# State-space stage of a four-layer decoder: C is applied by ScalarE per token between two turns by TensorE, for 160 of 256 units

## The chip, the core and the metric

The kernel runs on one core of a Trainium2 chip (trn2). The metric is the device time of one execution in microseconds (us). The core has a matrix engine (TensorE, PE in the profile, its weight loads PEld), VectorE (DVE), ScalarE (ACT), GpSimd (POOL) and SyncE (SP), which here issues the DMAs. Each works through its own list of instructions in order and is coupled to the others by semaphores. TensorE writes to PSUM only; GpSimd does not read PSUM here.

## The reference

A decoder with four layers on x of 32 sequences x 64 tokens x 256 features (2048 tokens). Each layer adds an attention-like block, a second one and a feed-forward block to x. The change is in the first block of the third layer, a selective state-space block with 512 inner channels, 16 states per channel and a convolution over four tokens:

```python
dA = exp(A[None, :, None, :] * dt[:, :, :, None])
dBu = dt[:, :, :, None] * Bm[:, None, :, :] * hs[:, :, :, None]
def step(h, inp):
    dA_t, dBu_t, C_t = inp
    h = dA_t * h + dBu_t
    y = einsum('bdn,bn->bd', h, C_t)
    return (h, y)
y = y + hs * D[None, :, None]
y = y * silu(gate)
return einsum('bdl,hd->blh', y, Wout)
```

So for each channel d and state n there is a recurrence over the 64 tokens of a sequence; the state is multiplied by C of its token and of n, and summed over the 16 n.

## The kernel before

The function is `l2_attn` (L1415). Tokens are cut into four chunks q of 512 (8 sequences), the 512 channels into four groups c of 128 partitions. A **unit** u is one state n of one channel group of one chunk: a tile of 128 channels x 512 tokens. There are 4 x 4 x 16 = 256 units. 32 units make a **half** k (two channel groups cc = 0, 1 that alternate, 16 states), two halves a chunk; `split` (L1501) gives (k, n, cc).

For a unit: ScalarE makes the decay `da` = exp(dt x A) into PSUM (`decay`, L1617), GpSimd the input `ub` = dtu x B (L1721), with B copied to all partitions in `bcn` by a DMA from `bct`. VectorE runs the recurrence as one scan (L1783 or L1788). Then the state is multiplied by C, which is the other half of `bcn`. `pooled` (L1505) chooses who does it: for 80 units the scan writes SBUF (`hb`) and GpSimd multiplies (`product`, L1710, `hp`); for 176 the scan writes PSUM (`ph`), and VectorE, having waited for its own scan, multiplies into `hc` (L1792). In an even half 12 of 32 units are pooled, in an odd one 8. TensorE sums over n by a matmul with the identity that accumulates in `py` (L1608). After 16 states VectorE adds the skip term (`skip`, L1773), GpSimd multiplies by the gate (L1701).

The order of each engine is written out by `schedule` (L1518), which all engines call: before unit u it places the jobs that the table `AT` puts at this position of the chunk (0 to 63), shifted by each engine's own `after`. Jobs: H, the projection and convolution of the next chunk (TensorE at 2, 5, 8, 11; ScalarE and VectorE 5 later, three VectorE instructions each); O, the output projection of the last chunk (TensorE 14 and 17); S, silu of four tiles and of the gate on ScalarE with two loads of its tables (20), before which it makes the decays of units 20 to 23 into the SBUF tile `dx`; X, the projection to dt, B and C (TensorE 23 and 25); D, softplus of dt (31 to 40, GpSimd 8 later); Z, the gate's projection (43 to 52). In the first chunk Z and D jobs stand at the places of Y and O. The job X 1 writes B and C to `bcs`, which SP stores to DRAM for `bcn`.

How far the engines run ahead: `ub` has four buffers, so GpSimd's `ub` of unit u waits for scan u - 4; `product` of unit u is placed after `ub` of u + 2 and waits for scan u. ScalarE's decay of u waits for scan u - 2. `bcn` has four buffers, and SP waits for all that read one before it loads it again. `bank` (L1497) gives jobs one of two PSUM banks `pp` in turn.

Of the kernel before, what the change touches and what calls it, by code (L numbers as in the profile page):

```python
# [17 lines left out]
ALU = mybir.AluOpType  # L18
# [1396 lines left out]
def l2_attn(nc, g, a):  # L1415
# [4 lines left out]
    NB, NUB, NHC, NDX = 4, 4, 4, 4  # L1420
    NU = NQ * IC * N
    with ExitStack() as ctx:
# [11 lines left out]
        def early(sp):  # L1434
            for dst, n in loads:
# [12 lines left out]
        bcs = s.sb("bcs", [2 * N, CH])  # L1448
# [4 lines left out]
        hc = [s.sb(f"hc{k}", [P, CH]) for k in range(NHC)]  # L1453
# [10 lines left out]
         hc_ready, hp_ready, add_done, skip_done, zs_ready, yz_ready, o_ready) = s.sem(  # L1464
            "a_exp", "pp0_free", "pp1_free", "raw_ready", "tap_ready", "conv_ready", "hs_ready", "z_ready",
            "x_ready", "dtin_ready", "bc_ready", "bc_stored", "d_ready", "sp_ready", "m_ready", "dt_ready", "dtu_ready", "da_ready",
            "ub_ready", "scan_done", "hc_ready", "hp_ready", "add_done", "skip_done", "zs_ready", "yz_ready", "o_ready")
# [46 lines left out]
        by_dve = [u for u in range(NU) if not pooled(u)]  # L1514
        pool_count = [sum(x <= u for x in by_pool) for u in range(NU)]
        dve_count = [sum(x <= u for x in by_dve) for u in range(NU)]

        def schedule(job, unit, skip, after):  # L1518
# [3 lines left out]
            for u in range(NU):  # L1522
# [14 lines left out]
        with nc.Block() as block:  # L1537

            @block.sync
            def _(sp):  # L1540
# [7 lines left out]
                for i in range(NU // 2):  # L1548
# [5 lines left out]
                    if i >= NB:  # L1554
                        last = 2 * (i - NB) + 1
                        sp.wait_ge(ub_ready, last + 1)
                        sp.wait_ge(hc_ready, dve_count[last])
                        if pool_count[last]:
                            sp.wait_ge(hp_ready, pool_count[last])
# [3 lines left out]
            def _(pe):  # L1563
                pe.wait_ge(w_loaded, nl)

                def job(q, j):
# [12 lines left out]
                    elif kind == "X":  # L1579
# [4 lines left out]
                        mm.then_inc(x_ready, 1)  # L1584
                    elif kind == "D":
# [11 lines left out]
                def unit(u):  # L1597
                    k, n, cc = split(u)
                    if pooled(u):
                        pe.wait_ge(hp_ready, pool_count[u])  # L1600
                        src = hp[(pool_count[u] - 1) % 2]
                    else:
                        pe.wait_ge(hc_ready, dve_count[u])
                        src = hc[(dve_count[u] - 1) % NHC]
# [3 lines left out]
                    pe.matmul(py[:, turn_ % 2, :], g.ident[:, :], src[:, :], start=n == 0, stop=n == N - 1).then_inc(add_done, 1)  # L1608
# [4 lines left out]
            def _(act):  # L1613
# [9 lines left out]
                def job(q, j):  # L1623
# [19 lines left out]
                    elif kind == "X":  # L1643
# [4 lines left out]
                        else:  # L1648
                            if q:
                                act.wait_ge(bc_stored, 32 * q)  # L1650
                            act.activation(bcs[:, :], out[0:2 * N, :], ACT.Copy).then_inc(bc_ready, 1)
# [31 lines left out]
                schedule(job, unit, lambda t: None, {"H": 5, "X": 4, "D": 6, "Z": 5})  # L1683

            @block.gpsimd
            def _(pool):
# [39 lines left out]

                schedule(job, unit, gated, {"D": 8, "skip": 3})

            @block.vector
            def _(dve):  # L1730
# [44 lines left out]
                def unit(u):  # L1775
                    i = u // 2
                    dve.wait_ge(da_ready, u + 1)
                    dve.wait_ge(ub_ready, u + 1)
                    if pooled(u):
# [3 lines left out]
                        dve.tensor_tensor_scan(hb[m % 2][:, :], factor(u), ub[u % NUB][:, :], 0.0, ALU.mult, ALU.add).then_inc(scan_done, 1)  # L1783
# [1487 lines left out]
```

## Time and profile before

| | |
|---|---|
| median of 3 runs | 4679.01 us (4669.22 to 4682.99) |
| profiled execution | 4676.15 us, its span 4674.4 us |
| TensorE, weight loads | 3974.4 us (85%), 2613.4 us (56%) |
| VectorE, ScalarE, GpSimd | 3124.8 us (67%), 2221.0 us (48%), 1513.6 us (32%) |
| state-space units | 922.3 to 1462.2 us of the span |

Shares are those of the whole span; the stage that is changed is 540 us of it. PEclk in the rows below is the granted clock of TensorE, with 1.00 for 2.4 GHz and 0.5 for 1.2 GHz. In answers by line, "idle before" is the idle time of that engine just before such instructions, and the name behind the arrow ended it.

### The profile page before, as it was taken

The page shows a single profiled execution, that of the slowest core. Times are in us where ns is not written, and L with a number is a line of the kernel's source. Part 1 is how long each engine was busy: PE and PEld are TensorE (multiplying, and loading weights), DVE is VectorE, ACT ScalarE, POOL GpSimd, SP SyncE. Part 2 cuts the span into 40 slices and gives each one's busy share as a digit, 9 for nine tenths or more (in the row PEclk, how much of TensorE's full clock was granted, in tenths as well). Part 3 has the DMA queues.
Part 4 walks back from the last instruction along what each step waited for, and adds up shares of the span by engine and source line. Part 5 has one row for each costly group of instructions (what it writes and reads, how often), then busy time and mean ns, then how long its engine had stood idle before and what let it go on. Part 6 is the DMA issues. An engine that isn't in the chain of part 4 may idle for free. (4 is left out here: it accounts for less than half of the span.)

```text
span 4674.4 us, 143172 instructions
## 1 busy us (share of the span) xinstructions
PE 3974.4 (85%) x62052; PEld 2613.4 (56%) x62052; DVE 3124.8 (67%) x5769; ACT 2221.0 (48%) x4151; POOL 1513.6 (32%) x1605
## 2 busy tenths in 40 slices
PE   7627886677766887999899999999999998689999
PEld 6415654323324665344577777777777776355555
DVE  7897744788887887765577777777777776521111
ACT  3446532654443555322566666666666665221111
POOL 1001100088895221000444444444444442112222
PEclk9858997889998999999899999999999998789999
DMA  1000000133332000100200000001000000041111
GB/s 35 19 27 11 2 13 21 47 114 122 127 129 79 2 2 22 34 1 1 51 22 25 22 22 25 22 22 26 22 26 24 22 13 4 7 135 53 54 50 43
DMA packets 72969, 175.13 MB, mean 37 GB/s; under 512 B 14578, under 2 KB 27892, under 8 KB 69748
## 3 DMA queue, kind: packets, MB, share of 16 engines
q1 hardware_dynamic: 72340, 165.96, 11.3%
q8 instruction: 490, 8.03, 0.7%
q14 instruction: 139, 1.14, 0.1%
HBM read 163.04 MB, written 2.88 MB: 35 GB/s over the span
## 5 line engine op out<-in xcount | busy, mean ns | idle before, releaser
L1721 POOL TENSOR_TENSOR ssm_ub<-ssm_dtu,ssm_bcn 128x512 f32<-128x512 f32 x256 | 325.1, 1299 | 300.0 <-DMA ssm_bcn<-ssm_bct 297.6
L3085 DVE TENSOR_TENSOR moe_hh<-moe_si,moe_pu 128x512 f32<-128x512 f32 x104 | 71.4, 687 | 450.6 <-PE moe_pu L2974 444.3
L2526 POOL TENSOR_TENSOR dn_gm<-dn_cb,dn_cs 128x256 f32<-128x256 f32 x128 | 76.9, 622 | 670.1 <-DMA dn_cb<-dn_cum 439.1
L1620 ACT ACTIVATE ssm_da<-core_XN,ssm_al 128x504 f32<-128x504 f32 x240 | 163.2, 683 | 255.6 <-DVE ssm_ph L1788 169.9
L3018 ACT ACTIVATE moe_si<-moe_pg 128x512 f32<-128x512 f32 x104 | 62.1, 597 | 467.5 <-PE moe_pg L2974 467.5
L2542 POOL TENSOR_TENSOR dn_eb<-dn_ee,dn_cc 128x512 f32<-128x512 f32 x64 | 66.8, 1044 | 647.6 <-DVE dn_cc L2652 647.6
L3037 POOL TENSOR_TENSOR moe_hw<-moe_hh,moe_cb 128x512 f32<-128x512 f32 x100 | 126.8, 1268 | 444.1 <-DVE moe_hh L3085 393.6
L1608 PE MATMUL ssm_py<-ssm_hc,core_ident 128*128 128x512 f32 x352 | 200.0, 671 | 66.4 <-DVE ssm_hc L1792 35.8
L2293 PE MATMUL dn_po<-dn_wo,dn_cT 128*128 128x256 f32 x1024 | 244.8, 393 | 2.3 <-ACT dn_cT L2460 2.2
L2208 PEld LDWEIGHTS dn_pm<-dn_XB,dn_mb 32*32 32x32 f32 x16384 | 166.7, 105 | 113.3 <-issue 110.0
L2208 PE MATMUL dn_pm<-dn_zz,dn_XB 32*32 32x32 f32 x16384 | 209.3, 195 | 23.5 <-issue 23.5
L1788 DVE TENSOR_TENSOR_SCAN ssm_ph<-ssm_da,ssm_ub 128x512 f32<-128x512 f32 x168 | 205.0, 1220 | 29.9 <-POOL ssm_ub L1721 17.5
L347 POOL TENSOR_TENSOR a_ke<-a_qkT,a_kmask 128x512 f32<-128x512 f32 (+1 forms) x96 | 86.0, 917 | 411.2 <-DVEq L637 303.0
L2293 PEld LDWEIGHTS dn_po<-dn_wo,dn_cT 128*128 128x128 f32 x1024 | 194.1, 195 | 30.9 <-ACT dn_cT L2460 3.3
L2208 PE MATMUL dn_pm<-dn_XB,dn_mb 32*32 32x32 f32 x16384 | 196.9, 194 | 10.6 <-issue 9.0
L2974 PE MATMUL moe_pg<-core_XT,moe_w 128*128 128x512 f32 x416 | 198.4, 600 | 0.0
L2208 PEld LDWEIGHTS dn_pm<-dn_zz,dn_XB 32*32 32x32 f32 x16384 | 180.6, 104 | 28.6 <-issue 28.5
L2974 PE MATMUL moe_pu<-core_XT,moe_w 128*128 128x512 f32 x416 | 195.6, 592 | 0.0
L2989 PE MATMUL moe_py<-moe_w,moe_hw 128*128 128x256 f32 x800 | 188.7, 379 | 0.0
L2989 PEld LDWEIGHTS moe_py<-moe_w,moe_hw 128*128 128x128 f32 x800 | 152.0, 190 | 62.5 <-issue 46.9
L2557 POOL TENSOR_TENSOR dn_mb<-dn_BD,dn_small 128x256 f32<-128x256 f32 x256 | 178.8, 734 | 0.0
L560 ACT ACTIVATE a_sc<-a_sc 128x1024 f32<-128x1024 f32 (+1 forms) x128 | 121.2, 947 | 119.6 <-DVE a_sc L665 56.9
(504 smaller groups left out, 10527.2 us busy)
## 6 DMA issues: line engine op xcount, KB each, us to landing
ssm_bcn<-ssm_bct SPq DMA_DIRECT2D x128, 512.0 KB, 3.6
dn_cb<-dn_cum SPq DMA_DIRECT2D x32, 512.0 KB, 4.8
dn_w<-in_dn_w SPq DMA_DIRECT2D x32, 388.0 KB, 3.4
moe_cb<-moe_rows SPq DMA_DIRECT2D x64, 192.0 KB, 2.8
moe_w<-in_moe_w SPq DMA_DIRECT2D x26, 384.0 KB, 7.3
moe_cb<-moe_rows SPq DMA_DIRECT2D x64, 128.0 KB, 3.0
dn_wo<-in_dn_w SPq DMA_DIRECT2D x16, 256.0 KB, 5.9
moe_cb<-moe_rows SPq DMA_DIRECT2D x64, 64.0 KB, 2.6
```

Source lines behind the costliest of these rows:

```text
L347: last = pool.tensor_tensor(dst[:, c, :, :], bcm(src[:, c, :], R), bc(kmask[:, :], P), ALU.mult)
L560: act.activation(flat(sc[par][:, 2 * h:2 * h + 2, :]), flat(sc[par][:, 2 * h:2 * h + 2, :]), ACT.Exp, scale=sl)
L1608: pe.matmul(py[:, turn_ % 2, :], g.ident[:, :], src[:, :], start=n == 0, stop=n == N - 1).then_inc(add_done, 1)
L1620: act.activation(nb(factor(u))[:, :, 1:S], nb(dt[q % 2][:, c, :])[:, :, 1:S], ACT.Exp, scale=al[:, n, c:c + 1]).then_inc(da_ready, 1)
L1721: pool.tensor_tensor(ub[u % NUB][:, :], dtu[q % 2][:, c, :], bcn[i % NB][:, 0, :], ALU.mult).then_inc(ub_ready, 1)
L1788: dve.tensor_tensor_scan(ph[:, m % 2, :], factor(u), ub[u % NUB][:, :], 0.0, ALU.mult, ALU.add).then_inc(scan_done, 1)
L2208: mm = pe.matmul(bank[r, n * HB:(n + 1) * HB], left(n, r), right(n, r), start=True, stop=True, tile_position=(q * HB, q * HB))
L2293: mm = pe.matmul(po[:, j // 2, (j % 2) * D:(j % 2 + 1) * D], cT[:, h * TPC + j, :], wo[e // NCH % 2][:, h, :], start=h == 0, stop=h == 1)
L2557: last = pool.tensor_tensor(halves(mb[i % 2][:, l - 1, :]), BD[:, :, :], bcm(small[:, 1 + l, :], NS), ALU.mult)
L2974: mm = pe.matmul(dst[:, m % 2, :], w[:, k, at:at + P], g.XT[:, kc, n * CH:(n + 1) * CH], start=kc == 0, stop=kc == DC - 1)
L2989: mm = pe.matmul(py[:, j, 0:D], h[:, j * P:(j + 1) * P], w[:, k, DC * 2 * P:], start=k == 0, stop=k == G - 1)
L3037: pool.tensor_tensor(hw[m % 3][:, :], hh[m % 3][:, :], cb[j % NCB][:, :], ALU.mult).then_inc(hw_ready, 1)
```

## The change

160 units are now "turned" and 96 pooled (in each half those with number 0, 1, 4, 7, ... 31: `r < 2 or r % 3 == 1`). For a turned unit the scan writes one of two SBUF tiles `hu`. TensorE turns it (four 128x128 transposes into `ph`, so tokens lie on partitions), ScalarE copies it to SBUF in four pieces with C as the per-partition scale (`ht`, two buffers), and TensorE turns it back and sums in one step: four matmuls with the scaled piece as the stationary operand and the identity as the moving one, accumulating in `py`. C by tokens comes from a new job C in each chunk (TensorE at 28, ScalarE 4 later): four transposes of `bcs`, which is now 128 partitions high and cleared once by GpSimd, and a copy to `ct`. TensorE's unit u first turns u and then sums u - 2; ScalarE's unit u makes the decay of u and then scales u - 2. VectorE has no product any more. The skip is one unit later. The DMA queue no longer waits for `hc`.

```diff
         def pooled(u):
-            k, n, cc = split(u)
-            return cc == 1 and (n % 4 != 0 if k % 2 == 0 else n % 2 == 0)
+            r = u % (2 * N)
+            return r < 2 or r % 3 == 1
...
-                    if k and u % (2 * N) == 3 + cc + after.get("skip", 0):
+                    if k and u % (2 * N) == 4 + cc + after.get("skip", 0):
...
+                def turned(u):
+                    m = turn_count[u] - 1
+                    pe.wait_ge(scan_done, u + 1)
+                    if m >= 2:
+                        pe.wait_ge(ht_ready, m - 1)
+                    for j in range(TPC):
+                        mm = pe.transpose(ph[:, m % 2, j * P:(j + 1) * P], hu[m % NHU][:, j * P:(j + 1) * P], g.ident[:, :])
+                    mm.then_inc(turned_done, 1)
+                def summed(u):
...
+                    m = turn_count[u] - 1
+                    pe.wait_ge(ht_ready, m + 1)
+                    for j in range(TPC):
+                        mm = pe.matmul(py[:, cc, j * P:(j + 1) * P], ht[m % NHT][:, j * P:(j + 1) * P], g.ident[:, :],
+                                       start=False, stop=n == N - 1 and j == TPC - 1)
+                    mm.then_inc(add_done, 1)
+                def unit(u):
+                    if not pooled(u):
+                        turned(u)
+                    if u >= 2:
+                        summed(u - 2)
...
+                def scaled(u):
+                    if u < 0 or pooled(u):
+                        return
+                    k, n, cc = split(u)
+                    m = turn_count[u] - 1
+                    act.wait_ge(turned_done, m + 1)
+                    if m >= NHT:
+                        act.wait_ge(add_done, by_turn[m - NHT] + 1)
+                    for j in range(TPC):
+                        last = act.activation(ht[m % NHT][:, j * P:(j + 1) * P], ph[:, m % 2, j * P:(j + 1) * P], ACT.Copy,
+                                              scale=ct[k // 2 % 2][:, j, n:n + 1])
+                    last.then_inc(ht_ready, 1)
                 def unit(u):
+                    ahead_of(u)
+                    scaled(u - 2)
...
                     else:
-                        m = dve_count[u] - 1
-                        if m >= 2:
-                            dve.wait_ge(hc_ready, m - 1)
-                        dve.tensor_tensor_scan(ph[:, m % 2, :], factor(u), ub[u % NUB][:, :], 0.0, ALU.mult, ALU.add).then_inc(scan_done, 1)
-                        if m >= NHC:
-                            dve.wait_ge(add_done, by_dve[m - NHC] + 1)
-                        dve.wait_ge(scan_done, u + 1)
-                        dve.tensor_tensor(hc[m % NHC][:, :], ph[:, m % 2, :], bcn[i % NB][:, 1, :], ALU.mult).then_inc(hc_ready, 1)
+                        m = turn_count[u] - 1
+                        if m >= NHU:
+                            dve.wait_ge(turned_done, m - NHU + 1)
+                        dst = hu[m % NHU]
+                    dve.tensor_tensor_scan(dst[:, :], factor(u), ub[u % NUB][:, :], 0.0, ALU.mult, ALU.add).then_inc(scan_done, 1)
```

## Rows read from the trace of the kernel before

**Rows 1.** Busy us of each engine in windows cut at the skips, us from span's start.

```profile
922.30:1003.00 80.70, 60.67 (x118) 22.95 (x118) 68.08 (x72) 40.00 (x58) 69.09 (x54) 0.86 0.36 119
1003.00:1070.00 67.00, 45.48 (x86) 16.45 (x86) 57.60 (x64) 31.69 (x48) 62.77 (x51) 0.91 0.35 129
1070.00:1140.10 70.10, 55.13 (x130) 24.88 (x130) 63.75 (x69) 31.68 (x45) 59.32 (x46) 0.94 0.34 118
...
1207.40:1279.50 72.10, 56.65 (x130) 24.80 (x130) 63.80 (x69) 31.59 (x45) 59.33 (x46) 0.92 0.32 115
...
1346.40:1407.20 60.80, 41.09 (x96) 18.36 (x96) 54.61 (x57) 26.06 (x36) 58.42 (x45) 0.92 0.38 135
1407.20:1462.20 55.00, 39.24 (x64) 12.96 (x64) 50.93 (x56) 18.49 (x27) 46.96 (x39) 0.86 0.33 115
sum 539.90, PE 390.51 PEld 153.95 DVE 473.82 ACT 242.85 POOL 481.40; mean PE 48.81 PEld 19.24 DVE 59.23 ACT 30.36 POOL 60.17
```

In each window the columns are its length, then PE, PEld, DVE, ACT and POOL, the granted clock, DMA share and GB/s.

**Rows 2.** Groups by line in 917 to 1462 us, shapes kept apart, VectorE.

```profile
L1788 DVE TENSOR_TENSOR_SCAN ssm_ph<-ssm_da,ssm_ub 128x512 f32<-128x512 f32 x168 | 205.0, 1220 | 29.9 <-POOL ssm_ub L1721 17.5 <-issue 11.2 <-ACT ssm_da L1620 1.1
L1792 DVE TENSOR_TENSOR ssm_hc<-ssm_ph,ssm_bcn 128x512 f32<-128x512 f32 x176 | 121.8, 692 | 19.1 <-DVE ssm_ph L1788 1.4
L1783 DVE TENSOR_TENSOR_SCAN ssm_hb<-ssm_da,ssm_ub 128x512 f32<-128x512 f32 x72 | 87.5, 1215 | 10.4 <-ACT ssm_da L1620 4.6 <-POOL ssm_ub L1721 4.0 <-issue 1.9
```

**Rows 3.** GpSimd's waits for scans in an even window (1070 to 1140.1) and an odd one.

```profile
POOL ssm_hp L1710 <- DVE ssm_hb L1783: 11.6, 5, 3.3
...
POOL ssm_hp L1710 <- DVE ssm_hb L1783: 1.9, 3, 0.7
```

**Rows 4.** Order of time in a quiet stretch: start us, us, engine, what.

```profile
1047.86 4.96 POOL L1721 TENSOR_TENSOR ssm_ub<-ssm_dtu,ssm_bcn 128x512 f32<-128x512 f32 x4
...
1050.33 1.22 DVE L1788 TENSOR_TENSOR_SCAN ssm_ph<-ssm_da,ssm_ub 128x512 f32<-128x512 f32 x1
...
1052.26 1.21 DVE L1783 TENSOR_TENSOR_SCAN ssm_hb<-ssm_da,ssm_ub 128x512 f32<-128x512 f32 x1
...
1053.39 1.21 DVE L1788 TENSOR_TENSOR_SCAN ssm_ph<-ssm_da,ssm_ub 128x512 f32<-128x512 f32 x1
```

**Rows 5.** Order of time: an X job (512 columns), transposes, f32 matmuls of 128 columns.

```profile
1119.63 3.60 PE L1583 MATMUL ssm_pp<-ssm_hs,ssm_wx 128*128 128x512 f32 x8
...
2345.52 0.80 PEld L2279 LDWEIGHTS dn_po<-core_ident,dn_cn 128*128 128x128 f32 x7 [0.29 <-issue]
...
21.53 1.86 PEld L378 LDWEIGHTS a_pm<-core_XT,a_wqk 128*128 128x128 f32 x16 [1.06 <-ACTq L579]
```

**Rows 6.** Groups of activations by line, shapes kept apart.

```profile
L2475 ACT ACTIVATE dn_sqr<-dn_bC 128x128 f32<-128x128 f32 x64 | 17.8, 277 | 44.9 <-PE dn_bC L2315 44.8
L1628 ACT ACTIVATE ssm_acc<-ssm_pp,ssm_vec 128x512 f32<-128x512 f32 x13 | 8.8, 679 | 6.0 <-PE ssm_pp L1577 6.0
L1666 ACT ACTIVATE ssm_zs<-ssm_pp 128x512 f32<-128x512 f32 x16 | 9.3, 583 | 4.0 <-PE ssm_pp L1577 4.0
L1620 ACT ACTIVATE ssm_dx<-core_XN,ssm_al 128x504 f32<-128x504 f32 x16 | 10.1, 699 | 0.0
```

**Rows 7.** Order of time: a convolution on VectorE and the scan after it.

```profile
942.99 2.34 DVE L1747 SCALAR_TENSOR_TENSOR ssm_acc<-ssm_pp,ssm_vec,ssm_acc 128x504 f32<-128x504 f32 x3
945.64 1.23 DVE L1788 TENSOR_TENSOR_SCAN ssm_ph<-ssm_da,ssm_ub 128x512 f32<-128x512 f32 x1 [0.31 <-POOL ssm_ub L1721]
```

**Rows 8.** Order of time: first and last part of a silu job on ScalarE.

```profile
1106.25 2.52 ACT L1620 ACTIVATE ssm_dx<-core_XN,ssm_al 128x504 f32<-128x504 f32 x4
...
1114.46 1.28 ACT L1642 ACT_TABLE_LOAD   x1
```

**Rows 9.** Order of time: an output job on TensorE.

```profile
1106.90 3.62 PE L1594 MATMUL ssm_pp<-ssm_wout,ssm_yy 128*128 128x256 f32 x16
```

**Rows 10.** Busy us in two windows, columns as in the first group.

```profile
965.00:985.00 20.00, 12.06 (x18) 4.46 (x18) 13.76 (x13) 15.05 (x20) 16.47 (x11) 0.66 0.23 79
1106.00:1122.00 16.00, 12.41 (x37) 6.67 (x36) 14.44 (x15) 11.67 (x15) 12.83 (x8) 1.00 0.28 99
```

More of the change, by code:

```diff
@@ L1419, in l2_attn @@
     NQ = TOK // CH
-    NB, NUB, NHC, NDX = 4, 4, 4, 4
+    NB, NUB, NHU, NHT, NDX = 4, 4, 2, 2, 4
     NU = NQ * IC * N
@@ L1447, in l2_attn @@
         dtin = s.sb("dtin", [P, CH])
-        bcs = s.sb("bcs", [2 * N, CH])
+        bcs = s.sb("bcs", [P, CH])
+        ct = [s.sb(f"ct{k}", [P, TPC, N]) for k in range(2)]
         bcn = [s.sb(f"bcn{k}", [P, 2, CH]) for k in range(NB)]
@@ L1452, in l2_attn @@
         hb = [s.sb(f"hb{k}", [P, CH]) for k in range(2)]
-        hc = [s.sb(f"hc{k}", [P, CH]) for k in range(NHC)]
+        hu = [s.sb(f"hu{k}", [P, CH]) for k in range(NHU)]
+        ht = [s.sb(f"ht{k}", [P, CH]) for k in range(NHT)]
         hp = [s.sb(f"hp{k}", [P, CH]) for k in range(2)]
@@ L1513, in l2_attn @@
         by_pool = [u for u in range(NU) if pooled(u)]
-        by_dve = [u for u in range(NU) if not pooled(u)]
+        by_turn = [u for u in range(NU) if not pooled(u)]
         pool_count = [sum(x <= u for x in by_pool) for u in range(NU)]
-        dve_count = [sum(x <= u for x in by_dve) for u in range(NU)]
+        turn_count = [sum(x <= u for x in by_turn) for u in range(NU)]
         def schedule(job, unit, skip, after):
@@ L1556, in _ @@
                         sp.wait_ge(ub_ready, last + 1)
-                        sp.wait_ge(hc_ready, dve_count[last])
                         if pool_count[last]:
@@ L1584, in job @@
                         mm.then_inc(x_ready, 1)
+                    elif kind == "C":
+                        pe.wait_ge(bc_ready, q + 1)
+                        if q == 0:
+                            pe.wait_ge(bcs_zeroed, 1)
+                        for j in range(TPC):
+                            mm = pe.transpose(out[:, j * P:(j + 1) * P], bcs[:, j * P:(j + 1) * P], g.ident[:, :])
+                        mm.then_inc(c_ready, 1)
                     elif kind == "D":
@@ L1650, in job @@
                                 act.wait_ge(bc_stored, 32 * q)
-                            act.activation(bcs[:, :], out[0:2 * N, :], ACT.Copy).then_inc(bc_ready, 1)
+                            else:
+                                act.wait_ge(bcs_zeroed, 1)
+                            act.activation(bcs[0:2 * N, :], out[0:2 * N, :], ACT.Copy).then_inc(bc_ready, 1)
+                        act.drain().then_inc(free, 1)
+                    elif kind == "C":
+                        out, free, uses = bank(q, j)
+                        act.wait_ge(c_ready, q + 1)
+                        act.activation(ct[q % 2][:, :, :], out.rearrange("p (j r) -> p j r", j=TPC)[:, :, N:2 * N], ACT.Copy)
                         act.drain().then_inc(free, 1)
@@ L1681, in unit @@
                     decay(u)
-                schedule(job, unit, lambda t: None, {"H": 5, "X": 4, "D": 6, "Z": 5})
+                schedule(job, unit, lambda t: None, {"H": 5, "X": 4, "C": 4, "D": 6, "Z": 5})
             @block.gpsimd
@@ L1725, in unit @@
                         product(u)
+                pool.memset(bcs[:, :], 0.0).then_inc(bcs_zeroed, 1)
                 schedule(job, unit, gated, {"D": 8, "skip": 3})
```

32 lines of the change are left out of this document (18 added, 14 removed).

## The prediction

> **What bounds the kernel now.** I began with the busy time of each engine in the state-space stage, cut where VectorE runs the skip of a half (unit 3 of the next half) [rows 1]. The reader should see two engines near their limit and two with room: over the 539.9 us from the first `ub` to the last skip GpSimd is busy 481.4 us and VectorE 473.8, TensorE 390.5, ScalarE 242.9. The even windows, with convolution, silu and output jobs, have VectorE above GpSimd (63.8 against 59.3 of 70.1 us); the odd ones, with the softplus jobs, have GpSimd above VectorE (62.8 against 57.6 of 67.0). Next came the groups by line [rows 2]: 176 products `hc` take 121.8 us of VectorE, 256 scans about 320. Then what GpSimd waits for [rows 3]: 11.6 us in an even window, always a scan whose product it must make, and 1.9 in an odd one. Last, a quiet stretch in order of time [rows 4]: a scan whose product VectorE makes takes 1.93 us until the next scan starts (1050.33 to 1052.26), a scan alone 1.13 (1052.26 to 1053.39); four `ub` take 4.96 us with the last one's tail, a pitch of 1.23. So the stage is bound by VectorE in even windows and by GpSimd in the softplus part of odd ones. Removing VectorE work pays at most in the first kind.
>
> **What goes, comes and moves.** VectorE loses all 176 products and the waits on its own scan: a turned unit's scan now costs 1.13 us instead of 1.93. The scans write SBUF where 168 wrote PSUM; those that already do so last 1.215 us against 1.220 [rows 2], so I cost that at nothing. VectorE's work falls by about 16 us a half and it no longer bounds an average half.
>
> GpSimd gains 16 products (96 for 80), 16 x 1.23 = 20 us. Where they land matters. In an odd window there were 7 and will be 12: +5 x 1.23 = 6.1. An even window had 13 and gets 12: -1.2. The first gets one more, the last (28 units) two more.
>
> TensorE: a unit had two instructions of 512 columns; eight such take 3.60 us with the last one's tail, so I take 0.43 each and 0.86 a unit [rows 5]. Now it has four transposes and four f32 matmuls of 128 columns. Seven transposes' weight loads span 0.80 us, a pitch of 0.11, so four take 0.44 (result after some 0.75); sixteen loads of f32 matmuls of this form span 1.86 us, also 0.11, and the four are eight instructions, 0.89. Together 1.33 us, +0.47, so 160 x 0.47 = 75 us of work on an engine with 149 us of idle time, all at full clock.
>
> ScalarE: 640 scalings of 128x128 from PSUM with a per-token scale. No row has this form. Without a scale operand it is 277 ns; 128x512 from PSUM costs 679 with one and 583 without, so the operand adds 0.09; I take 0.37 us each. Chained activations overlap: four of 0.699 take 2.52 [rows 8], so by 0.09 each. Four scalings are then 4 x 0.37 - 3 x 0.09 = 1.21 us, 1.12 of occupation [rows 6]. Bounds: 4 x 0.277 - 0.27 = 0.84, and without overlap 1.48. In all 160 x 1.12 = 179 us beside 242.9: ScalarE becomes 78% busy. What VectorE did for a unit in 0.69 us ScalarE does in 1.21. The Trainium skill (ScalarE: Activation LUTs, Rules for kernel authors) says to put `mul` on VectorE, not ScalarE; counted product for product that rule would give +160 x 0.52 = +83 us, some 4762. The rows do not support adding it up like that, since ScalarE idles for half of every window.
>
> Small edits: GpSimd's clearing of `bcs` sits in its 297 us of idle time before the first `ub`; the four C jobs add four transposes and a 0.6 us copy each, beside GpSimd work; the DMA queue loses a wait. Nothing.
>
> **Where the waits go.** In a quiet run of three units (two turned, one pooled) the demands are GpSimd 4 x 1.23 = 4.9 us, ScalarE 3 x 0.63 + 2 x 1.12 = 4.1, TensorE 2 x 1.33 + 0.86 = 3.5, VectorE 3.4. GpSimd bounds; an odd window becomes 62.8 + 6.1 + 1.2 of issue gaps and semaphore waits + 0.5 at the skip = 70.6 us, against 66.9 to 67.3: +3.5 in each of three. The last window: 47.0 + 2.5 + some 3.8 at the end = 53.3 against 55.0, -1.7.
>
> Even windows. (a) A convolution takes 2.65 us of VectorE (942.99 to 945.64) [rows 7] before each of four pooled scans, so three units need 3.4 + 2.65 = 6.05 us of VectorE against 4.9 of GpSimd. GpSimd must wait at each product; the first wait is covered by its lead of two units, the other three are 1.2 each: 3.6. (b) The silu job keeps ScalarE 9.5 us (1106.25 to 1115.74) [rows 8], and now the scalings of two older units queue behind it. From the end of scan 17: TensorE turns unit 17 only after the second output job, 3.6 us [rows 9]; the turned state is there at 3.4, scaled at 4.6; silu until 14.1; unit 18 scaled at 15.3, unit 20 at 16.4; unit 21 could be turned only after the sum of unit 18, so it is scaled at 18.1; then the decay of unit 24 at 18.8 and scans 24 and 25 end at 20.0 and 21.1. GpSimd comes to the product of unit 25 at 16.1 and waits 5.0. (c) Two X jobs of 3.6 us [rows 5] stand in TensorE's queue before units 23 and 25; the turns behind them hold ScalarE's scalings and with them the next decays. Carried on in the same way GpSimd loses 5 us more up to unit 33. In all 3.6 + 10 + 1 at the skip = 14.6 us, where it waited 11.6 (and about the same 2 us more in the other such window). So 59.3 - 1.2 + 14.6 = 72.7 against 70.1 and 72.1: +2.6 and +0.6. The first window has Z jobs instead of output jobs: 69.1 + 1.2 + 0.5 + 12.6 = 83.4 against 80.7, +2.7. The seventh has neither convolution nor X: 58.4 - 1.2 + 4 = 61.2 against 60.8, +0.4.
>
> Sum: 2.7 + 3 x 3.5 + 2.6 + 0.6 + 0.4 - 1.7 = +15 us. (d) TensorE would idle about 8 us while it waits for unit 18's scaling. In the window 965 to 985, where it waited in the same place, the granted clock was 0.66, with stretches at 1.2 GHz; in the corresponding 1106 to 1122, where it kept its sums coming, it was 1.00 at 2.4 GHz [rows 10]. Half clock would hit the X jobs: 3.4 us lost for 6.8 us at half clock, of which GpSimd's four buffers hide part; I take 2 us in each of three: +6. Bounds 0 and +15. Total +21. The profiled execution took 4676.2 us (2.8 under the median of 4679.0), so it would take 4697; against the median, 4700.
>
> **Rivals.** *Unchanged waits.* The gates above are loose by a microsecond each; if GpSimd's waits and gaps stay near 45 us (58.5 now), the stage takes 501 + 45 = 546, +6: 4685. For it: GpSimd runs up to four units ahead. Against: ScalarE's queue order, with scalings behind silu, is fixed. *Faster.* With VectorE off the path only GpSimd's own work remains: 481.4 + 19.6 + 20 of ends, gaps and convolution waits = 521, -19: 4660. It needs the silu job and the X jobs to be hidden by the lead of GpSimd; the point is total waits under about 25 us. The old even windows, where these jobs cost VectorE only some 2.6 us of idle time, speak for it; that a turned unit now makes three more hand-overs between engines before its buffer is free speaks against. *ScalarE bounds.* If small activations do not overlap, three units cost 3 x 0.69 + 2 x 1.48 = 5.0 us plus jobs, above GpSimd; some 0.4 us a triple and longer silu tails give +55: 4735. *TensorE at half clock.* Its work is 160 x 1.33 + 96 x 0.86 + some 105 of jobs = 400 us at full clock; with half clock for 60% of the work it needs 640 and sets the stage: +100, 4780. The matmuls proper in three units fall little, from 2.6 us in some 5.3 to 2.6 in 4.9, so rows do not show a reason. The Trainium skill (TensorE: Matmul & The Clock Gate, Part 4: PE-mode transpose) says that transposes do not count as activity for the clock; no stretch here is pure enough to test that, and by it this rival would be the likelier the more time goes to turns.
>
> **How the numbers follow.** About 0.3% (14 us) is what a measurement of this kernel can tell from no change. Forecast (coupled queues, 4700) 0.42; ScalarE or TensorE as the bound 0.10; unchanged waits 0.34; faster 0.14. The time is the forecast's. The range takes in the unchanged case, the near end of faster (4665), the unlucky ends of (b) to (d) and ScalarE's case: 4665 to 4742; that leaves out most of faster and the half-clock case. Slower 0.52, same 0.34, faster 0.14.
>
> **What would show it.** GpSimd busy near 501 us of a stage of about 561; its waits for scans in even windows about 15 us, longest (5 us) after the silu job; odd windows near 70.6 us; VectorE busy about 350; a scaling 0.37 us; turns with a pitch of 0.11; a TensorE wait of some 8 us for scaled states in each silu job, with a lower granted clock after it. It would be wrong if odd windows stay at 67, if the waits vanish, or if TensorE or ScalarE is without idle time in the quiet stretches.

## The result and the profile after

The changed kernel takes 4711.6 us (median of 5 runs, 4704.7 to 4719.8) against 4679.0 (5 runs, 4664.6 to 4683.0): ratio 1.0071, with 95% between 1.0052 and 1.0090, so 33 us slower. The forecast was 4700 and its range 4665 to 4742. Whether the way there was the forecast one is another matter, and the windows answer it.

The first part of the page, busy time of each engine, of the changed kernel; its profiled execution took 4711.6 us with a span of 4709.8:

```profile
PE 4027.0 (86%) x63660; PEld 2776.6 (59%) x63668; DVE 3018.6 (64%) x5593; ACT 2383.1 (51%) x4795; POOL 1529.6 (32%) x1622
```

The same windows as in [rows 1], of the changed kernel, cut at the first skip of each half, with the same columns:

```profile
919.80:1028.50 108.70, 75.39 (x324) 47.33 (x324) 56.43 (x51) 60.78 (x143) 70.17 (x54) 0.84 0.26 89
1028.50:1096.60 68.10, 54.05 (x288) 39.25 (x288) 41.86 (x38) 52.55 (x129) 66.71 (x56) 0.92 0.37 124
1096.60:1169.40 72.80, 61.80 (x332) 44.21 (x332) 51.95 (x50) 51.92 (x126) 60.56 (x48) 0.93 0.34 117
1169.40:1237.40 68.00, 51.49 (x288) 36.57 (x288) 41.91 (x38) 52.44 (x129) 66.62 (x55) 0.97 0.36 124
1237.40:1309.80 72.40, 61.36 (x332) 44.06 (x332) 51.98 (x50) 51.92 (x126) 60.56 (x48) 0.95 0.35 118
...
1377.80:1441.00 63.20, 51.27 (x296) 41.24 (x296) 43.22 (x37) 46.12 (x115) 57.51 (x48) 0.89 0.40 134
1441.00:1493.60 52.60, 40.32 (x260) 31.73 (x260) 37.05 (x33) 38.31 (x104) 50.48 (x42) 0.96 0.37 121
sum 573.80, PE 445.74 PEld 319.79 DVE 366.29 ACT 406.47 POOL 499.22; mean PE 55.72 PEld 39.97 DVE 45.79 ACT 50.81 POOL 62.40
```

The stage grew by 33.9 us, from 539.9 to 573.8, which is all of the loss. Of that 28.0 lie in the first window (80.7 to 108.7) and 5.9 in the other seven. The busy sums are what was expected of a change that moves work: GpSimd 499 us, VectorE 366, ScalarE 406. In the first window no engine is near its limit: TensorE is busy 75 and GpSimd 70 of 109 us. That points to engines that wait for each other in a ring rather than to one that bounds. In the odd windows GpSimd is now the bound (66.7 of 68.1).

The groups of the changed kernel by line, shapes kept apart:

```profile
L1716 ACT ACTIVATE ssm_ht<-ssm_ph,ssm_ct 128x128 f32<-128x128 f32 x640 | 182.4, 376 | 97.6 <-PE ssm_ph L1611 96.4
L1846 DVE TENSOR_TENSOR_SCAN ssm_hu<-ssm_da,ssm_ub 128x512 f32<-128x512 f32 x148 | 179.9, 1219 | 94.0 <-ACT ssm_da L1650 79.3 <-POOL ssm_ub L1778 12.9 <-PE ssm_ph L1611 1.2
```

A scaling lasts 376 ns. The scans stand idle 79 us for decays, and the reason is one line up: ScalarE, which makes the decays, stands 96 us in front of a scaling until TensorE has turned the state. Where? The waits in the first window:

```profile
ACT ssm_ht L1716 <- PE ssm_ph L1611: 41.7, 12, 6.6
DVE ssm_hu L1846 <- ACT ssm_da L1650: 41.3, 14, 5.2
...
POOL ssm_hp L1767 <- DVE ssm_hb L1846: 25.2, 7, 6.2
...
PE ssm_pp L1578 <- DVEq L1808: 11.1, 3, 3.7
```

And one round of it in order of time:

```profile
949.83 3.63 PE L1578 MATMUL ssm_pp<-core_XT,ssm_win 128*128 128x512 f32 x4 [3.69 <-DVEq L1808]
949.96 1.23 DVE L1846 TENSOR_TENSOR_SCAN ssm_hb<-ssm_da,ssm_ub 128x512 f32<-128x512 f32 x1 [0.32 <-issue]
...
951.26 1.26 POOL L1767 TENSOR_TENSOR ssm_hp<-ssm_hb,ssm_bcn 128x512 f32<-128x512 f32 x1 [6.10 <-DVE ssm_hb L1846]
...
953.30 0.60 PE L1611 MATMUL ssm_ph<-core_ident,ssm_hu 128*128 128x128 f32 x4
...
953.94 1.14 ACT L1716 ACTIVATE ssm_ht<-ssm_ph,ssm_ct 128x128 f32<-128x128 f32 x4 [6.62 <-PE ssm_ph L1611]
...
955.43 0.71 ACT L1650 ACTIVATE ssm_da<-core_XN,ssm_al 128x504 f32<-128x504 f32 x1
...
955.62 1.98 PE L1578 MATMUL ssm_pp<-core_XT,ssm_win 128*128 128x512 f32 x4 [0.82 <-ACT ssm_zs L1703]
...
956.17 1.22 DVE L1846 TENSOR_TENSOR_SCAN ssm_hu<-ssm_da,ssm_ub 128x512 f32<-128x512 f32 x1 [4.99 <-ACT ssm_da L1650]
...
960.97 2.33 DVE L1805 SCALAR_TENSOR_TENSOR ssm_acc<-ssm_pp,ssm_vec,ssm_acc 128x504 f32<-128x504 f32 x3
...
963.48 3.64 PE L1578 MATMUL ssm_pp<-core_XT,ssm_win 128*128 128x512 f32 x4 [3.69 <-DVEq L1808]
```

The first chunk has Z jobs between the H jobs (TensorE at 2 H, 3 Z, 5 H, 6 Z, ...), and jobs take the two `pp` banks in turn. So H 1 needs the bank of H 0 (in later chunks it is H 2 that does), and VectorE frees that only with its convolution, which stands before unit 7 in its own order. TensorE has H 1 before unit 5 and so stops there. Now follow the rows: the job starts when the convolution has ended (949.83), and the turn of the unit that has its place behind the job ends 4 us later (953.30 and 0.60); ScalarE's scaling of that unit had stood at the head of its queue for 6.6 us; the next decay comes only behind it (955.43), so VectorE's scan starts at 956.17, idle for 5.0; and the next convolution, which frees the next bank, stands behind that scan (960.97). Each convolution thus waits for the job that waited for the one before. From one such job to the next three units take 13.65 us (949.83 to 963.48), where the kernel before took 7.64 (942.99 [rows 7] to its next convolution at 950.63).

The clock takes a part of each round. The four matmuls that start at 949.83 take 3.63 us, the four of the same form at 955.62 take 1.98. Windows of the changed kernel around the first of them, columns as above, show the granted clock at 0.53, near the 1.2 GHz level, behind the wait of 3.69 us, and at 1.00 (2.4 GHz) in the next stretch:

```profile
949.80:953.40 3.60, 3.57 (x5) 1.51 (x6) 1.23 (x1) 0.00 (x0) 2.14 (x2) 0.53 0.03 5
953.40:957.60 4.20, 3.38 (x19) 2.18 (x18) 1.22 (x1) 2.20 (x6) 1.70 (x3) 1.00 0.32 125
```

So some 1.65 us of the 13.65 (3.63 less 1.98) are the slower clock, and they lie on the ring, since the turn stands behind this job.

### The profile page after: what moved, and what is told of

Same layout as the page of the kernel before. It is cut to its first block and busy times, and to the rows that moved or that the text cites. A ratio compares the mean times of both kernels' runs of the same rounds, so it can differ in the third digit from the quotient of the medians.

```text
span 4709.8 us, 147050 instructions
## 1 busy us (share of the span) xinstructions
PE 4027.0 (86%) x63660; PEld 2776.6 (59%) x63668; DVE 3018.6 (64%) x5593; ACT 2383.1 (51%) x4795; POOL 1529.6 (32%) x1622
## 5 line engine op out<-in xcount | busy, mean ns | idle before, releaser
L2596 POOL TENSOR_TENSOR dn_eb<-dn_ee,dn_cc 128x512 f32<-128x512 f32 x64 | 66.7, 1042 | 651.3 <-DVE dn_cc L2706 651.3
L1846 DVE TENSOR_TENSOR_SCAN ssm_hu<-ssm_da,ssm_ub 128x512 f32<-128x512 f32 x148 | 179.9, 1219 | 94.0 <-ACT ssm_da L1650 79.3
L2262 PEld LDWEIGHTS dn_pm<-dn_XB,dn_mb 32*32 32x32 f32 x16384 | 166.6, 105 | 110.9 <-issue 107.5
L1716 ACT ACTIVATE ssm_ht<-ssm_ph,ssm_ct 128x128 f32<-128x128 f32 x640 | 182.4, 376 | 97.6 <-PE ssm_ph L1611 96.4
L1627 PEld LDWEIGHTS ssm_py<-core_ident,ssm_ht 128*128 128x128 f32 x1280 | 170.2, 201 | 68.2 <-issue 40.1
L1627 PE MATMUL ssm_py<-core_ident,ssm_ht 128*128 128x128 f32 x1280 | 177.5, 285 | 26.0 <-ACT ssm_ht L1716 26.0
```

The lines of the kernel that those rows point to most:

```text
L1627: mm = pe.matmul(py[:, cc, j * P:(j + 1) * P], ht[m % NHT][:, j * P:(j + 1) * P], g.ident[:, :], start=False, stop=n == N - 1 and j == TPC ...
L1716: last = act.activation(ht[m % NHT][:, j * P:(j + 1) * P], ph[:, m % 2, j * P:(j + 1) * P], ACT.Copy, scale=ct[k // 2 % 2][:, j, n:n + 1])
L1846: dve.tensor_tensor_scan(dst[:, :], factor(u), ub[u % NUB][:, :], 0.0, ALU.mult, ALU.add).then_inc(scan_done, 1)
L2262: mm = pe.matmul(bank[r, n * HB:(n + 1) * HB], left(n, r), right(n, r), start=True, stop=True, tile_position=(q * HB, q * HB))
```

## The experiments

Eleven kernels, all measured against the kernel before. The ratios are taken over the repeated runs, the stage and the windows are of one profiled execution of each kernel. Window lengths are cut as above: first, second (odd), third (even), seventh.

| kernel | pooled | ratio (95%) | stage us | first | 2nd | 3rd | 7th |
|---|---|---|---|---|---|---|---|
| before | 80 | 1 | 539.9 | 80.7 | 66.9 | 70.2 | 60.8 |
| changed | 96 | 1.0071 (1.0052 to 1.0090) | 573.8 | 108.7 | 68.1 | 72.8 | 63.2 |
| e1 Z jobs ahead | 96 | 1.0015 (1.0002 to 1.0028) | 547.3 | 82.4 | 68.0 | 72.7 | 63.2 |
| e2 the same in before | 80 | 1.0004 (0.9993 to 1.0016) | 543.5 | 82.3 | 66.9 | 72.2 | 60.8 |
| e3 turn first | 96 | 1.0018 (1.0004 to 1.0031) | 552.8 | 91.2 | 68.0 | 72.9 | 60.2 |
| e4 scalings in silu | 96 | 1.0049 (1.0032 to 1.0067) | 562.5 | 105.5 | 68.0 | 68.7 | 63.2 |
| e5 before, new set | 96 | 1.0033 (1.0020 to 1.0046) | 553.2 | 83.5 | 66.9 | 76.3 | 60.3 |
| e7 e1+e3+e4 | 96 | 0.9973 (0.9961 to 0.9985) | 531.6 | 81.2 | 68.0 | 67.1 | 60.2 |
| e8 e7, fewer | 72 | 0.9989 (0.9972 to 1.0006) | 532.4 | 83.9 | 65.4 | 70.1 | 58.6 |
| e9 e7, fewer in odd | 84 | 0.9976 (0.9959 to 0.9993) | 523.5 | 81.4 | 65.7 | 66.1 | 60.2 |
| e10 e7, shifted | 96 | 0.9994 (0.9983 to 1.0005) | 538.5 | 83.2 | 68.0 | 67.8 | 61.8 |
| e11 e5, shifted | 96 | 1.0005 (0.9995 to 1.0016) | 546.1 | 81.2 | 67.0 | 74.5 | 60.6 |
| e12 e9, shifted even | 84 | 0.9977 (0.9965 to 0.9989) | 528.4 | 83.4 | 65.7 | 67.8 | 61.2 |

### Is it the bank ring? e1 and e2

e1 does the four Z jobs of the first chunk before unit 0, as the H jobs already are, and changes nothing else; e2 does that to the kernel before, as a control.

```diff
-        ahead = [("H", 0), ..., ("X", 1), ("D", 1), ("C", 0)]
+        ahead = [("H", 0), ..., ("X", 1), ("D", 1), ("C", 0), ("Z", 0), ("Z", 1), ("Z", 2), ("Z", 3)]
...
-        AT.update({("Y", c): 3 + 3 * c for c in range(IC)})
```

> The changed kernel, with the four gate projections of the first chunk (Z jobs of chunk 0) done before unit 0 instead of between units 3 and 12. Theory A (ring through the PSUM banks): in the first half TensorE comes to the projection H 1 at unit 5 and needs the bank that VectorE's convolution of H 0 frees only before unit 7; the turn of unit 5 is queued behind it, ScalarE's scaling behind the turn, the decay of unit 8 behind the scaling. Without the Z jobs the banks alternate over two more units, as in the later chunks, and the first half falls from 108.7 us to some 80 to 85: about 4686 us. Theory B (the first half simply has more TensorE work and a lower clock, 0.84): only the work of the Z jobs goes, four times 1.9 us, so at most 8 us: about 4704. Theory C (two buffers of hu and ht are too few): no change but those 8 us.

> The same edit in the kernel before, as a control. Theory A: TensorE waits for the banks there too, but only sums are queued behind, with four buffers of hc, so no ring closes: the first half falls from 80.7 us by the 3 to 6 us that TensorE's extra work cost at most, about 4674 us. Theory B: a similar gain in both kernels, some 8 us each.

e1: the first window falls from 108.7 to 82.4 us, the stage by 26.5, and the ratio from 1.0071 to 1.0015, which is 26 us. First its window, then its waits in the same place:

```profile
921.90:1004.30 82.40, 65.80 (x319) 43.28 (x317) 55.48 (x51) 61.28 (x144) 70.29 (x55) 0.88 0.34 117
```

```profile
DVE ssm_hu L1845 <- ACT ssm_da L1649: 13.4, 9, 4.0
...
ACT ssm_ht L1715 <- PE ssm_ph L1610: 11.8, 8, 4.5
POOL ssm_hp L1766 <- DVE ssm_hb L1845: 9.4, 7, 1.9
```

GpSimd does the same work (70.2 and 70.3 us), and the wait of `hu` scans for decays falls from 41.3 to 13.4. TensorE has less to do in the window, since the Z jobs, 16 matmuls that now take 7.0 us in one piece, run before it; e2 (no gain from the same move) and e3 (most of the gain without it) below show that this is not what was gained. The wait of `ssm_pp` for VectorE's queue is no longer among them. In order of time, turns of e1 with the H job between them, and two convolutions:

```profile
937.84 0.60 PE L1610 MATMUL ssm_ph<-core_ident,ssm_hu 128*128 128x128 f32 x4
...
941.36 1.88 PE L1577 MATMUL ssm_pp<-core_XT,ssm_win 128*128 128x512 f32 x4
...
943.08 0.60 PE L1610 MATMUL ssm_ph<-core_ident,ssm_hu 128*128 128x128 f32 x4
...
948.32 0.60 PE L1610 MATMUL ssm_ph<-core_ident,ssm_hu 128*128 128x128 f32 x4
...
949.01 2.33 DVE L1804 SCALAR_TENSOR_TENSOR ssm_acc<-ssm_pp,ssm_vec,ssm_acc 128x504 f32<-128x504 f32 x3
...
955.01 2.33 DVE L1804 SCALAR_TENSOR_TENSOR ssm_acc<-ssm_pp,ssm_vec,ssm_acc 128x504 f32<-128x504 f32 x3
```

TensorE passes three units in 5.24 us at first (937.84 to 943.08 to 948.32) and then settles to VectorE's round: from one convolution to the next it is 6.00 us (949.01 to 955.01) instead of 13.65. Four convolutions make three such rounds, so 3 x 7.65 = 23 of the 26.3 us that this window lost are explained by the round alone. It is the bank wait that set it. e2 shows that the edit is worth nothing by itself: in the kernel before the same wait existed, but only sums stood behind it on TensorE, and `hc` had four buffers. Of the kernel before:

```profile
953.15 1.98 PE L1577 MATMUL ssm_pp<-core_XT,ssm_win 128*128 128x512 f32 x4 [1.37 <-DVEq L1750]
```

I had expected 3 to 6 us from the first window of e2 and got 82.3 for 80.7, so no gain shows from removing the few `pp` waits there (3.9 us in three waits for convolutions). e2 says one more thing: its third window is 72.2 us where the kernel before had 70.2, though the edit does not reach it. A single window can thus differ by 2 us between two profiles.

### Is it the turn's place behind the job? e3

The wait for the bank can also be left alone if the turn goes ahead of the job in TensorE's order. Nothing else moves, and the buffers are the same.

```diff
-        def schedule(job, unit, skip, after):
+        def schedule(job, unit, skip, after, first=lambda u: None):
...
                 q, at = u // (IC * N), u % (IC * N)
+                first(u)
...
                 def turned(u):
+                    if pooled(u):
+                        return
...
-                    if not pooled(u):
-                        turned(u)
...
-                schedule(job, unit, lambda t: None, {})
+                schedule(job, unit, lambda t: None, {}, turned)
```

> The changed kernel, with TensorE's turn of unit u placed ahead of the jobs at u instead of behind them; the sum of u - 2 stays behind. Nothing else. Theory A: the bank wait no longer holds a turn, so the ring opens: first half from 108.7 us to 85 or 90, and the even halves lose 1 to 3 us each of waits behind O and X jobs; about 4685 us. Theories B and C: the work, clock and buffers are the same, so 4711 within 3 us.

The first window is 91.2 us: 17.5 of the 28 come back although the bank wait remains. Of e3, in the same stretch as above:

```profile
949.70 1.98 PE L1579 MATMUL ssm_pp<-core_XT,ssm_win 128*128 128x512 f32 x4 [1.53 <-DVEq L1809]
...
951.13 1.26 POOL L1768 TENSOR_TENSOR ssm_hp<-ssm_hb,ssm_bcn 128x512 f32<-128x512 f32 x1 [3.80 <-DVE ssm_hb L1847]
```

```profile
949.70:958.45 8.75, 7.22 (x35) 4.59 (x35) 5.66 (x6) 5.10 (x15) 4.95 (x4) 1.00 0.15 60
```

TensorE now waits 1.5 us for the bank where it waited 3.7, and GpSimd 3.8 where it waited 6.1; a round takes 8.75 us (turns at 943.66 and 952.41). The clock stays at 1.00 through the round, and the job behind the wait takes 1.98 us where it took 3.63, so up to 1.65 of the 4.9 us that each round gains come with the clock: e3 by itself does not separate it from the order. Both links, the bank and the place of the turn, belong to the ring, and cutting the bank wait (e1) cuts it best. The third link, ScalarE's scalings ahead of its decays, is read from the trace alone: no run moved it. The seventh window fell from 63.2 to 60.2, which was not expected; the gain expected in the other even windows didn't come (72.9 for 72.8): there something later in the half seems to take it up. e4 and e7 below fit that: with the silu job mended too, this edit is worth 1.6 and 2.6 us in these windows (67.1 and 66.1 in e7, 68.7 in e4).

### What holds the even windows: e4

The scalings of units 18, 20 and 21 stand behind the silu job. e4 puts them between its activations.

```diff
                             act.activation(zs[(q - 1) % 2][:, :, :], zs[(q - 1) % 2][:, :, :], ACT.Silu).then_inc(zs_ready, 1)
+                            base = (q - 1) * IC * N + silu_at
+                            scaled(base - 2, True)
...
                                 act.activation(hs[q % 2][:, k, :], acc[:, k, :], ACT.Silu, bias=tap(K, k)).then_inc(hs_ready, 1)
+                                if q and k in (1, 3):
+                                    scaled(base + k // 2, True)
...
-                def scaled(u):
-                    if u < 0 or pooled(u):
+                def scaled(u, now=False):
+                    if u < 0 or pooled(u) or (u in early and not now):
```

> The changed kernel, with ScalarE's scalings of the pending units (18, 20, 21 of each chunk) put between the silu activations instead of behind the whole silu job. Theory S (GpSimd's 4.2 us wait after the silu job comes from the scalings queued behind it): that wait and TensorE's 7.5 us wait for scaled states go, 3 to 4 us in each of four chunks: about 4698 us. Rival: the wait only moves to the two X jobs of TensorE that come next, so at most 1 us a chunk: 4708.

The silu job in the changed kernel, in order of time:

```profile
1129.63 2.54 ACT L1650 ACTIVATE ssm_dx<-core_XN,ssm_al 128x504 f32<-128x504 f32 x4
...
1137.85 1.28 ACT L1672 ACT_TABLE_LOAD   x1
1139.15 2.17 ACT L1716 ACTIVATE ssm_ht<-ssm_ph,ssm_ct 128x128 f32<-128x128 f32 x8
...
1140.34 2.07 PE L1627 MATMUL ssm_py<-core_ident,ssm_ht 128*128 128x128 f32 x8 [7.49 <-ACT ssm_ht L1716]
...
1145.05 1.22 DVE L1846 TENSOR_TENSOR_SCAN ssm_hu<-ssm_da,ssm_ub 128x512 f32<-128x512 f32 x1 [6.48 <-ACT ssm_da L1650]
...
1147.47 1.26 POOL L1767 TENSOR_TENSOR ssm_hp<-ssm_hb,ssm_bcn 128x512 f32<-128x512 f32 x1 [4.15 <-DVE ssm_hb L1846]
```

Eight scalings in a row at 1139.15 end a wait of 7.5 us of TensorE, and GpSimd's product pays 4.15. In e4 the same stretch reads:

```profile
1132.74 1.91 ACT L1665 ACTIVATE ssm_zs<-ssm_zs 128x2048 f32<-128x2048 f32 x1
1134.56 1.12 ACT L1725 ACTIVATE ssm_ht<-ssm_ph,ssm_ct 128x128 f32<-128x128 f32 x4
1135.56 1.34 ACT L1676 ACTIVATE ssm_hs<-ssm_acc,ssm_vec 128x512 f32<-128x512 f32 x2
...
1135.73 1.22 PE L1627 MATMUL ssm_py<-core_ident,ssm_ht 128*128 128x128 f32 x8 [3.61 <-ACT ssm_ht L1725]
```

The even windows fall from 72.8 and 72.4 to 68.7, the stage by 11.3 us and the ratio by 0.0022, 10 us. So the scalings behind silu are worth some 4 us in each, as much as GpSimd's wait there. The expectation had four chunks of 3 to 4 us and 4698; it came to 4695.9, with 3.2 us in the first window and nothing in the seventh.

### Is the new set of pooled units to blame? e5 and e11

e5 is the kernel before with the new choice of pooled units alone; e11 the same with the choice one place earlier, so that the products stand elsewhere beside the convolutions.

```diff
         def pooled(u):
-            k, n, cc = split(u)
-            return cc == 1 and (n % 4 != 0 if k % 2 == 0 else n % 2 == 0)
+            r = u % (2 * N)
+            return r < 2 or r % 3 == 1
```

(e11: `r % 3 == 0`.)

> The kernel before, with only the new choice of pooled units (96 for 80, the products of the other 160 still on VectorE). It measures the share that GpSimd's extra work has by itself. By the prediction's terms GpSimd gains 16 x 1.23 = 20 us, nearly all in odd halves, where VectorE, which loses 16 x 0.8 = 13 us, is not the bound during the softplus jobs but is elsewhere: +1 to +4 us in each odd half, 0 to -2 in the even ones, about 4682 us. Rival: that GpSimd's work is hidden and VectorE's relief pays, about 4665.

> The kernel before with 96 pooled units in the shifted set 0, 1, 3, 6, ... 30 (products of the others on VectorE). With 0, 1, 4, 7, ... 31 its even halves grew from 70.2 and 72.1 us to 76.3 and 76.5, although the number of products there was the same, 12. If the convolutions before pooled scans are the cause, they go back to 70 to 73 and the kernel to about 4680. If it is the pooling of both channel groups in turn (sums of both wait for GpSimd), they stay at 76.

Both missed. In e5 the odd windows don't move (66.9 and 67.2) although a half of them has 12 products instead of 8, and the even ones grow by 6.1 and 4.4 us, to 76.3 and 76.5, where a half has 12 in both. The even window of e5 and its waits:

```profile
1078.00:1154.00 76.00, 60.49 (x130) 25.94 (x130) 64.38 (x70) 31.48 (x45) 60.64 (x47) 0.87 0.32 112
```

```profile
ACT ssm_da L1620 <- DVE ssm_hb L1783: 18.9, 8, 3.9
...
POOL ssm_hp L1710 <- DVE ssm_hb L1783: 15.4, 7, 3.4
```

VectorE's work is what it was [rows 1], and GpSimd waits 15.4 us for scans where it waited 11.6 [rows 3]. The shift of e11 brings back some 2 us (74.5 and 73.9), no more than a window can differ between profiles; in the ratios, 1.0033 and 1.0005, the shift is clearer. What makes the rest was not found. What e5 does show: had VectorE kept its product for the other 160 units, the new set by itself would cost 13 us of stage, and the changed kernel with its ring cured (e1) stands at 547.3 against e5's 553.2. With this set TensorE and ScalarE in VectorE's place are therefore no loss. Against the shifted set (e11, 546.1) they are no gain either.

### The cures together, and the number of pooled units: e7 to e10, e12

e7 is e1, e3 and e4 at once; its e4 part names unit 19 too, which is pooled in e7 but turned in some of the others. The rest change its choice of pooled units alone:

```diff
-            return r < 2 or r % 3 == 1
+            return r < 2 or r % 4 == 1                                # e8
+            return r < 2 or r % (4 if u // (2 * N) % 2 else 3) == 1   # e9
+            return r < 2 or r % 3 == 0                                # e10
```

e12 is e9 with `r % 3 == 0` in even halves.

> The changed kernel with the three edits together: Z jobs of the first chunk ahead, the turn ahead of the jobs, scalings between the silu activations. If the ring and the silu queue are what the change costs, their gains add except where the first two open the same ring: 29.5 and 30.3 us share most, the third gives 15.7, so 4711.6 - 31 - 15 = 4665, and GpSimd is left as the bound with waits under 15 us. If another engine had become the bound underneath, it stays at or above 4675.

> As the one with all three edits, with 72 pooled units (0, 1, 5, 9, ... 29 of each half) and 184 turned. If GpSimd is the bound after the mends, 24 products less take 24 x 1.23 = 29 us off it, of which TensorE (24 x 0.47 = 11 us more) and ScalarE (24 x 1.14 = 27 us more) give some back in even halves: about 4650. If ScalarE and TensorE are level with GpSimd already, no gain or a loss: 4665 to 4680.

> As the one with all three edits, with the smaller pooled set in odd halves only (84 pooled, 172 turned). In odd halves GpSimd has the softplus jobs and bounds with 66.7 of 68 us, while ScalarE and TensorE wait: 12 products less, 12 x 1.23 = 15 us, should come off nearly in full: about 4651. In even halves nothing changes. If it equals the run with 72 pooled units, the even halves are bound by ScalarE and TensorE.

> As the one with all three edits and 96 pooled units, but the pooled ones are 0, 1, 3, 6, ... 30 instead of 0, 1, 4, 7, ... 31. The four convolutions of an even half stand before units 7, 10, 13, 16: with the old set each stands just before a pooled scan, whose product GpSimd waits for; now before a turned one. If that coincidence costs its waits (5.5 us of GpSimd in an even half of the run with all three edits), three of four even halves lose 2 to 4 us: stage 531.6 to some 522, about 4655. If the convolution is then only waited for at the next product: no change, 4663.

> All three edits, the shifted set in even halves and 0, 1, 5, 9, ... 29 in odd ones (84 pooled). By the stage of the runs so far (531.6 us with 96, 522.6 with 84) and 3 us less in each of three even halves: stage about 514 against 539.8 before, about 4652, so faster than the kernel before by 0.4 to 0.5%. If the shift gives nothing, 4660.

e7 beats both kernels: 4662.9 us, ratio 0.9973 (0.9961 to 0.9985). Its third window, and GpSimd's waits in it:

```profile
1072.50:1139.60 67.10, 62.94 (x335) 43.55 (x333) 51.81 (x51) 52.11 (x127) 60.53 (x48) 0.97 0.37 127
```

```profile
POOL ssm_hp L1777 <- DVE ssm_hb L1856: 5.5, 5, 1.5
```

GpSimd waits 5.5 us there for scans instead of 10.1, and TensorE is busy 62.9 of 67.1: it now stands level with GpSimd. TensorE also keeps its clock there: its wait in the silu job is 0.97 us. Fewer pooled units (e8) don't help in even windows: 70.1, with GpSimd busy only 55.5 us and more turns on TensorE (62.7) and ScalarE (55.1). None of them is at its limit, so it is the chain of turns that is likely longer; no run shows it. e8 missed: 4668 us where 4650 was expected. Fewer in odd windows alone (e9) do help: 68.0 to 65.7, and the stage is 523.5, 16 us under before. Its median doesn't show all of that (4662.1 where 4651 was expected; the ratio of 0.9976 is 11 us). The shifted sets (e10, e12) missed as well: their even windows are 67.8 against 67.1 and 66.1, and e10's ratio (0.9994) is above e7's (0.9973), so the place of the convolutions beside the products is not what is left there.

One reading limits all of this. The span minus the stage, which no edit touches but the one that puts the Z jobs ahead, was 4134.6 us in the profile of before, 4136.1 in that of the changed kernel, and between 4124.3 (e11) and 4149.3 (e8) in the others. Over the kernels that is a range of 25 us, so a gain of some 10 us in the stage can be lost in the whole. e7, e9 and e12 are each faster than before; which of them is best was not settled.

## Why the prediction was right, and where it was not

- **The sum and its sign.** 4711.6 against 4700, inside the range, and slower as forecast; the number was good by luck. Of the 33.9 us of stage, 28.0 lie in one window priced at +2.7, a term too small by 25.3. Without the ring (e1) the stage is +7.4, where the sum had +15 and 6 more for the clock. So two errors of opposite sign made the number look good.
- **The first window (+2.7, was +28.0): the failed step.** The text treated it as an even window with "Z jobs instead of output jobs". It took each job at its length and never asked which bank a job takes and who frees it. The bank waits were in the trace of before (the job of 1.98 us above that began when VectorE's queue had freed its bank) and cost nothing there, as e2 shows, since only sums stood behind them. The change put the turns there, and with ScalarE's scalings in front of its decays the wait went round. e1 and e3 show the bank and the turn's place as links; the link through ScalarE is in the rows (5.0 us of idle time of a scan until the decay that followed the scaling), without a run of its own. The slower clock behind each bank wait, some 1.65 us a round, was not in the term either. How the prediction came to 12.6 us of waits in this window it does not say.
- **Odd windows (+3.5 each, were +1.2, +0.7 and +1.1).** GpSimd bounds them, as said, with 1.4 us of idle time (68.10 less 66.71) where 1.7 was taken. Its busy time was too high: 68.9 expected, 66.7 measured. An odd half now has 54 GpSimd operations (32 `ub`, 12 products, 10 others), and 54 x 1.235 us is 66.7. Before it had 8 products, so 50 operations, which is 61.7; the window was busy 62.8 [rows 1], so it held about one more than its own. The sum took the 7 products that this window happened to hold and added five where four come (1.2 us), to a busy time with one too many (1.0 us). Products should have been counted by the rule in the code, not by the window.
- **Even windows (72.7 expected, 72.8 and 72.4).** Right in length, by terms that traded places; the base itself moved by 2 us between two profiles (e2), so the +2.6 of the first is not sharp. The terms: busy 60.6 where 58.1 was expected (an even half keeps its 12 products, so nothing was to be taken off, and the window holds 48 operations where 46 were), waits 12.3 (10.1 and 2.2) where 14.6 was. In order of time GpSimd waits 2.3 us at the products behind convolutions (3.6 expected; 0.2, 1.04 and 1.04), 4.15 behind the silu job (5.0), 5.8 from there to the end of the X jobs (5) and nothing at the skip (1). TensorE's wait for scaled states was 7.5 us (8).
- **Seventh window (+0.4, was +2.4), last (-1.7, was -2.4).** The seventh's excess is the turn behind its jobs, as e3 shows (60.2).
- **The clock (+6).** TensorE waited as foreseen, and the granted clock there was 0.68 where it had been 1.00 [rows 10]:

```profile
1129.00:1145.00 16.00, 7.97 (x41) 6.25 (x40) 8.19 (x5) 13.95 (x28) 14.32 (x9) 0.68 0.25 101
```

  The loss has the size of the term: from the end of the wait to the X job (1140.34 to 1145.45) TensorE needs 5.1 us for a turn and three sums that take 3.1 at full clock (0.44, 0.86 and twice 0.89), so 2.0. But it falls on these and not on the X jobs, which ran at 3.60 us each as before. e4 gives little of it back, though the clock of its even windows is 0.98 for 0.93. The same work behind the shorter wait takes 4.9 us (1135.73 to 1140.59) at a granted clock of 0.65:

```profile
1135.70:1140.60 4.90, 4.87 (x23) 3.83 (x24) 2.15 (x2) 4.88 (x13) 4.90 (x4) 0.65 0.12 35
```

  What rose is mostly the clock of the time in which TensorE waited (0.59 from 1132.8 to 1140.3 in the changed kernel), and that costs nothing. The half-clock rival fell: with 160 turned units the odd windows were granted 0.92, 0.97 and 0.97 (0.91, 0.88 and 0.91 before).
- **Costs.** A scaling 376 ns (0.37 taken), four in 1.14 us (1.21), GpSimd busy 499 us (501), a scan into SBUF 1219 ns (as before): these held. ScalarE gained 164 us (179), TensorE 55 (75). VectorE kept 366 us (350): its 121.8 us of products had in part overlapped their neighbours, and 107.5 left.
- **Rivals.** "Unchanged waits" had +6 of stage; with the first chunk cured it is +7.4, so that rival describes the stage without the ring better than the forecast does (+5.9 in the other seven windows, +12.3 in its sum). "Faster" needed the silu and X jobs to be hidden; they were not, though e4 and e7 show they can be in part. ScalarE was never the bound (406 of 574 us). The rule of the Trainium skill (ScalarE: Activation LUTs, Rules for kernel authors) that puts `mul` on VectorE was the ground for a time of 4762. In speed the trace agrees with it: 1.14 us for a unit on ScalarE against 0.69 on VectorE. But that time did not come on top where ScalarE has room; e7 is faster than the kernel before with all 640 scalings on ScalarE.

## What to carry to other kernels

When a step is moved into an engine's fixed order, list what that engine waits for just ahead of the new place, in the first round of the loop too, and follow each wait to the engine that ends it; if that one now needs the moved step, the waits form a ring, and its round can cost far more than any term of work (13.65 us here for three units of 6.00). A window in which every engine is a third idle is how it looked in this profile. Cutting one link of the ring was enough to bring back most of it. A helper copy in an in-order queue belongs between the long jobs, not behind them, and a window's busy time should be checked against its own count of operations before a term is added to it.

## What the hardware showed that was not expected

Transposes among f32 matmuls did not lower TensorE's clock. The Trainium skill (TensorE: Matmul & The Clock Gate, Part 4: PE-mode transpose) says that the full clock does not engage for transposes, since they do not count as busy in the same way. The odd windows, in each of which 20 units are now turned, were granted 0.92, 0.97 and 0.97 of full clock with TensorE busy 50 to 54 of 68 us, against 0.91, 0.88 and 0.91 before (45 to 47 of 67 us). With 23 turned in each (e9) it was 0.97, 0.97 and 0.95. Each turned unit has its f32 matmuls too, so this says that the mixture keeps the clock, not what transposes alone would do.

The same job shows in two kernels what a wait of TensorE can do to its clock: behind a bank wait of 3.69 us four matmuls took 3.63 us at a granted clock of 0.53, behind one of 1.53 us (e3) they took 1.98 at 1.00.

VectorE's scans and GpSimd's operations lengthened each other where the decay lies in SBUF (`dx`): in the even window of the changed kernel two of the four such scans took 2.22 us and the GpSimd operations beside them 2.17 to 2.19, where others take 1.22 and 1.27. One such scan with no GpSimd operation beside it, in the seventh window, took 1.19. The kernel before has the same lengths, 2.22 and 2.18.

Open: the 4 to 6 us by which the kernel before grows in each even window with the new set (e5, e11). Four `hu` buffers and another order of scaling and decay on ScalarE were not tried. More `hu` buffers would likely not have helped: scans waited 1.2 us in all for a turn to free one, and 79.3 for decays.
